# Block sums stored as one run per partition, row records loaded by word and turned on TensorE

## The chip, the cores and the metric

The kernel runs on one core of a Trainium2 chip. A core has TensorE (PE; its weight loads are listed as PEld), VectorE (DVE), ScalarE (ACT), GpSimd (POOL) and SyncE (SP, which here only issues DMAs), a scratch memory of 128 partitions (SBUF), the accumulators that TensorE writes (PSUM), and 16 DMA engines that all queues share. The metric is the device time of one execution in microseconds (us), the median of several runs; lower is better.

## The reference, cut to what matters

A graph layer on 6250 nodes and 200,000 edges sorted by destination, and then a small mixture of experts. Only the graph layer is touched by the change.

```python
def _L0_gnn_ref(x, W, a_src, a_dst, edge_W, edge_b, bias, edge_attr, edge_index):
    h = (x @ W.T).reshape(n, H, D)                       # H = 8 heads of D = 32
    src, dst = (edge_index[0], edge_index[1])
    h_src, h_dst = h[src], h[dst]
    alpha = jnp.einsum('ehd,hd->eh', h_src, a_src) + jnp.einsum('ehd,hd->eh', h_dst, a_dst)
    enc = jax.nn.relu(edge_attr @ edge_W.T + edge_b).reshape(-1, H, D)
    alpha = alpha + jnp.sum(enc * h_dst, axis=-1)
    alpha = jnp.where(alpha >= 0, alpha, 0.2 * alpha)
    amax = jax.ops.segment_max(alpha, dst, num_segments=n)
    ex = jnp.exp(alpha - amax[dst])
    denom = jax.ops.segment_sum(ex, dst, num_segments=n)
    attn = ex / jnp.maximum(denom[dst], 1e-10)
    out = jax.ops.segment_sum(h_src * attn[..., None], dst, num_segments=n)
    return out.reshape(n, H * D) + bias
x = x + _L0_gnn_ref(_layernorm(x), ...)
x = x + _L0_ffn_ref(_layernorm(x)[None], ...)[0]
```

## The kernel before

Four parts follow one another. `prologue` projects the nodes into a table in device memory (`t_node_rows`, 272 floats a node) and sorts the edges into rows of W = 4 slots, each row with edges of one destination. 128 rows make a block, there are 440 blocks. For each row it stores a record of five words: four source ids and the place of the row's node in a window of 128 nodes (`t_block_rows`, tile `ro`). `edge_loop` does the edges, `merge_blocks` joins the sums of nodes that lie in two blocks, `epilogue` fetches each node's sum, divides it and runs the experts.

`edge_loop` is what the change is about. It takes STEPS = 110 steps of Q = 4 blocks, and all its buffers have two slots (RING = 2), so that loads for step q+2 go into the slot that step q leaves. Each engine has its own program, written out by hand in the order in which it runs; they meet at semaphores alone.

- SP, in `body(q)`: `store(q-1)` (L813) writes the sums of the last step, 128 partitions x 4 blocks x 264 floats, after the last copy of sums on ACT (L982). Then `load(q+2)`: `load_rows` (L784, the records), `load_attr` (L792, three DMAs of edge attributes), `load_windows` (L807, four windows of the node table, each after a register load of its base) and `load_flags` (L800, four).
- POOL, in `gather(q)`: 16 indirect DMAs (L856), one for each block and slot, each of which fetches 128 rows of the node table by the ids in the record. The four of block b wait until the step before last has weighed its block b (L1077), for the buffer.
- ACT and PE make the nodes' rows for each block (`front`): ACT makes a one-hot matrix (L943, L947), PE turns it (L871), ACT copies it (L954), PE encodes the attributes (L880) and picks the nodes from the window (L885), ACT copies the result (L963). The next block's L943 stands behind this copy.
- DVE multiplies the encoded attributes with that copy (L1032), adds them up (L1036), makes the scores of the step (L1044 to L1052), runs two scans over the rows (L1059, L1064; PE turns the rows for them, L891, and back, L896), subtracts the tops (L1070), and weighs the gathered rows (L1077) once ACT has taken the exponential (L969).
- PE adds up the weighed rows for each block (`add_up`, L904, 4 of these a block), and ACT copies the sums (L982).

The two transfers that the change touches, and their access patterns, are these:

```python
rows = scr["block_rows"].rearrange("(n q) (r w) -> n r q w", q=Q, w=W + 1)
sp.dma_start(rec[:, q.par, :, :], v).then_inc(s_rec[q.par], 16)            # L784
rows = scr["sums"][0:BLOCKS * P, :].rearrange("(n q p) e -> n p q e", q=Q, p=P)
sp.dma_start(v, sums[:, q.par, :, :]).then_inc(s_stored[q.par], 16)        # L813
```

In both, a partition's four blocks lie apart in device memory. So one transfer is 128 x 4 = 512 pieces: of 5 words (20 bytes) in the record load, and of 264 floats (1056 bytes) in the store. A window's 128 pieces have 1088 bytes each.

Of the kernel before, what the change touches and what calls it, by code (L numbers as in the profile page):

```python
# [8 lines left out]
P = 128  # L9
# [98 lines left out]
def prologue(nc, a, scr, keep):  # L108

    with Scope(nc) as m:  # L110
# [21 lines left out]
        row_at = m.sb("row_at", [P, GROUPS])  # L132
        base = m.sb("base", [P, GROUPS])
        base_mod, base_tile = keep["base_mod"], keep["base_tile"]
        tiny = m.sb("tiny", [P, 4])
        ro = m.sb("ro", [P, P, W + 1])
# [57 lines left out]
            dummy_made dummy_stored bias_loaded""".split()  # L194
# [29 lines left out]
        def _(sp):  # L224
# [46 lines left out]
            for g in range(GROUPS):  # L271
# [3 lines left out]
                sp.dma_start(scr["block_rows"][b0:b0 + n, :], ro[0:n, :, :].rearrange("p r w -> p (r w)")).then_inc(s["table_stored"], 16)  # L275
# [17 lines left out]
        def _(pool):  # L293
# [7 lines left out]
            for g in range(GROUPS):  # L301
# [8 lines left out]
                           allow_small_or_imprecise_dtypes=True).then_inc(s["consts_made"], 1)  # L310
            nc.gpsimd.iota(block_f[:, :], pattern=[[P, GROUPS]], base=1, channel_multiplier=1,
# [173 lines left out]
        def _(dve):  # L485
# [116 lines left out]
            def expand(g):  # L602
# [36 lines left out]
                link(nc.vector.tensor_scalar(ro[:, :, 0:W].bitcast(I32), away.rearrange("p (r k) -> p r k", k=W), float(DUMMY), None, ALU.add))  # L639
# [7 lines left out]
                nc.vector.tensor_scalar(ro[:, :, W], place, -1.0, 1.0, ALU.mult, ALU.add)  # L647
# [23 lines left out]
            link(nc.vector.tensor_tensor(item_to[:, :, 1], item_to[:, :, 1], row_at[:, :], ALU.add))  # L671
            nc.vector.tensor_copy(item_i[:, :, 1], item_to[:, :, 1]).then_inc(s["items_made"], 1)
            nc.vector.tensor_copy(item_i[:, :, 0], row_at[:, :]).then_inc(s["items_made"], 1)
# [39 lines left out]
def edge_loop(nc, a, scr, keep):  # L713

    with Scope(nc) as m:
        rec = m.sb("rec_in", [P, RING, Q, W + 1])
        rec_i = rec[:, :, :, :].bitcast(I32)
# [25 lines left out]
        p_rowT, p_back = p_turn[0:Q * H, 0:P], p_turn[:, 2 * P:2 * P + Q * H]  # L743
        row_of = lambda v: v.rearrange("p (q h) -> p q h", q=Q)
# [7 lines left out]
        names = """waited_by_pe waited_by_pool ones_set apart hot turned hotT picked near enc prod dots raw full score row_top rowT run tops back below  # L752
# [1043 lines left out]
```

## Time and profile before

| | |
|---|---|
| Time, median of 3 runs | 4180.87 us (4165.67 to 4185.18) |
| The profiled execution: time, and span of the trace | 4159.17 us, 4157.4 us |
| Granted TensorE clock, mean | 0.734 |
| PE, PEld busy | 58%, 39% |
| DVE, ACT, POOL busy | 57%, 24%, 48% |
| DMA queue q0 (POOL's gathers), q1 (SP's and ACT's) | 25.6%, 14.8% of 16 engines' span |
| The loop of 110 steps | from about 399 to 3571 us |

Each row of a timeline is an instruction or a run of equal ones: start and duration in us, engine, line, operation, tiles, shapes, and in brackets how long the engine had been idle before it and what ended that. An "SPq" row is the issue of a DMA, not its data. PE's ends are modelled from its starts; when a result really was there is seen at the engine that waited for it. "remote" is a wait whose end came from an update that no instruction's recorded end explains.

### The profile page before, as it was taken

What the parts mean: (1) busy time and instruction counts of PE and PEld (TensorE: products, weight loads), DVE (VectorE), ACT (ScalarE), POOL (GpSimd) and SP (SyncE); (2) the same over time, 40 slices, a digit from 0 to 9 for tenths busy, and PEclk for the clock granted to TensorE, in tenths of its full rate; (3) what the DMA queues carried; (4) which work ended last, traced back from release to release, by engine and by line L of the source; (5) the groups of instructions that cost most, each with busy time, mean ns of one, the idle gap of its engine ahead of it and who ended that gap; (6) DMA issues with size and microseconds to landing.
All of it is one profiled execution on the core that took longest, in us unless ns stands there. A gap on an engine that the chain in (4) does not pass through costs nothing. (4 is left out here: it accounts for less than half of the span.)

```text
span 4157.4 us, 45593 instructions
## 1 busy us (share of the span) xinstructions
PE 2392.0 (58%) x8886; PEld 1609.8 (39%) x8886; DVE 2354.5 (57%) x3523; ACT 992.1 (24%) x3079; POOL 2016.2 (48%) x2041
## 2 busy tenths in 40 slices
PE   3300556566566565565565665665656656416998
PEld 2200334333343343343343343433433433204887
DVE  7596556556556565565565565565655555443223
ACT  4300222222222222222222222222222222124332
POOL 2411555565555555555555655655556555244200
PEclk9755677776777777777777777767767777656999
DMA  7201444444444444444444444444444498320000
GB/s 240 76 30 46 114 125 115 124 124 115 125 122 118 125 123 120 126 122 118 124 115 124 126 117 124 124 113 125 117 122 124 115 118 113 52 66 23 13 20 29
DMA packets 322416, 437.60 MB, mean 105 GB/s; under 512 B 115526, under 2 KB 257832, under 8 KB 322132
## 3 DMA queue, kind: packets, MB, share of 16 engines
q0 software_dynamic: 90000, 262.14, 25.6%
q1 hardware_dynamic: 231540, 174.91, 14.8%
q10 hardware_dynamic: 848, 0.26, 0.0%
q14 instruction: 21, 0.17, 0.0%
q8 instruction: 7, 0.11, 0.0%
HBM read 351.33 MB, written 85.74 MB: 105 GB/s over the span
## 5 line engine op out<-in xcount | busy, mean ns | idle before, releaser
L856 POOL DMA_INDIRECT src_in<-t_node_rows,rec_in x1760 | 1800.8, 1023 | 1369.2 <-DVE weighted L1077 806.8
L1032 DVE SCALAR_TENSOR_TENSOR prod<-p_enc,near 128x512 f32<-128x512 f32 x880 | 566.4, 685 | 1224.6 <-ACT near L963 734.1
L904 PE MATMUL p_sum<-weighted,hot 128*128 128x264 f32 x3520 | 1021.8, 453 | 34.4 <-DVE weighted L1077 34.2
L871 PE MATMUL p_pick<-ident,hot 128*128 128x128 f32 x440 | 162.6, 370 | 1310.6 <-ACT hot L947 883.0
L904 PEld LDWEIGHTS p_sum<-weighted,hot 128*128 128x128 f32 x3520 | 794.5, 229 | 284.5 <-issue 114.6
L871 PEld LDWEIGHTS p_pick<-ident,hot 128*128 128x128 f32 x440 | 68.5, 156 | 1467.8 <-ACT hot L947 1011.1
L1036 DVE TENSOR_REDUCE dots<-prod 128x32 f32<-128x1024 f32 x440 | 536.9, 1220 | 15.2
L885 PE MATMUL p_pick<-win,hotT 128*128 128x272 f32 x880 | 439.9, 593 | 160.3 <-issue 119.6
L1077 DVE TENSOR_TENSOR weighted<-src_in,weighted 128x1024 f32<-128x1024 f32 x440 | 521.8, 1226 | 0.4 <-ACT weighted L969 0.4
L963 ACT COPY near<-p_pick 128x272 f32<-128x272 f32 x440 | 169.9, 386 | 1246.6 <-remote 726.1
L982 ACT COPY sums<-p_sum 128x264 f32<-128x264 f32 x440 | 166.9, 379 | 780.7 <-PE p_sum L904 524.7
L880 PE MATMUL p_enc<-expander,attrT 30*128 30x256 bf16 x1760 | 349.8, 331 | 0.3 <-DMA attrT<-t_block_attr 0.3
L885 PEld LDWEIGHTS p_pick<-win,hotT 128*128 128x128 f32 x880 | 175.2, 249 | 294.8 <-issue 235.8
L943 ACT ACTIVATE apart<-node_at,rec_in 128x128 f32<-128x128 f32 x440 | 175.3, 398 | 255.7 <-DMA rec_in<-t_block_rows 255.7
L880 PEld LDWEIGHTS p_enc<-expander,attrT 30*128 30x128 bf16 x1760 | 170.9, 120 | 99.0 <-issue 54.2
L954 ACT COPY hotT<-p_pick 128x128 f32<-128x128 f32 x440 | 117.6, 267 | 369.4 <-PE p_pick L871 162.2
L1482 PE MATMUL p_up<-x2T,w 128*128 (+2 forms) x800 | 175.9, 379 | 9.0 <-DMA b<-in_L_ffn_b 9.0
L1492 PE MATMUL p_y<-w,act_h 128*128 128x256 f32 x784 | 173.2, 379 | 0.0
L1482 PEld LDWEIGHTS p_up<-x2T,w 128*128 128x128 f32 x800 | 151.4, 192 | 29.7 <-DMA b<-in_L_ffn_b 9.1
L1492 PEld LDWEIGHTS p_y<-w,act_h 128*128 128x128 f32 x784 | 148.9, 190 | 20.2
L1685 DVE TENSOR_TENSOR acc<-acc,p_y 128x256 f32 (+1 forms) x49 | 20.6, 421 | 218.6 <-PE p_y L1492 216.2
L947 ACT ACTIVATE hot<-apart 128x128 f32<-128x128 f32 x440 | 136.1, 309 | 23.2
(293 smaller groups left out, 1639.5 us busy)
## 6 DMA issues: line engine op xcount, KB each, us to landing
win<-t_node_rows SPq DMA_DIRECT2D x440, 136.0 KB
t_block_sums<-sums SPq DMA_DIRECT2D x110, 528.0 KB
src_in<-t_node_rows,rec_in POOLq DMA_INDIRECT x1760
attrT<-t_block_attr SPq DMA_DIRECT2D x330, 36.0 KB
flags_in<-t_block_flags SPq DMA_DIRECT2D x440, 4.0 KB
t_node_rows<-out_rows SPq DMA_DIRECT2D x49, 136.0 KB, 1.7
x<-in_x SPq DMA_DIRECT2D x4, 1536.0 KB, 25.7
out_x<-x SPq DMA_DIRECT2D x48, 128.0 KB
```

Source lines behind the costliest of these rows:

```text
L856: pool.indirect_dma_start(src[:, q.par, b, k, :], None, scr["rows"], bass.IndirectOffsetOnAxis(ap=rec_i[:, q.par, b, k:k + 1], axis=0)).th ...
L871: nc.tensor.transpose(p_hotT, hot[:, q.par, b, :], keep["ident"][:, :]).then_inc(s["turned"], 1)
L880: last = nc.tensor.matmul(p_enc[(PAIRS * b + half) % len(p_enc)][:, j, :], slots, keep["expander"][:, :], start=True, stop=True)
L885: nc.tensor.matmul(p_near, hotT[:, b % 2, :], win[:, q.par, b, :], start=True, stop=True).then_inc(s["picked"], 1)
L904: last = nc.tensor.matmul(p_sum[b % 2][:, 0:ROW], hot[:, q.par, b, :], weighted[:, b, k, :], start=(k == 0), stop=(k == W - 1))
L943: nc.scalar.activation(apart[:, :], keep["node_at"][:, :], ACT.Abs, bias=rec[:, q.par, b, W:W + 1]).then_inc(s["apart"], 1)
L963: nc.scalar.copy(near[:, q.par, b, :], p_near).then_inc(s["near"], 1)
L1032: nc.vector.scalar_tensor_tensor(prod[:, b % 2, 2 * half:2 * half + 2, :], p_enc[(PAIRS * b + half) % len(p_enc)][:, :, :], 0.0, near[:, q ...
L1036: nc.vector.tensor_reduce(dots[:, q.par, b, :, :].rearrange("p k h -> p (k h)"), prod[:, b % 2, :, :].rearrange("p k (h d) -> p (k h) d", ...
L1077: nc.vector.tensor_tensor(heads(weighted[:, b, :, 0:D]), heads(src[:, q.par, b, :, 0:D]), spread(weighted[:, b, :, D:ROW], HD), ALU.mult). ...
L1482: last = nc.tensor.matmul(p_up[n % 4][:, 0:cols], w1[:, k, i, f * P:(f + 1) * P], x, start=(i == 0), stop=(i == 1))
L1492: last = nc.tensor.matmul(p_y[u][:, :], act_h[:, b, n, u * P:(u + 1) * P], w2[:, k, f, :], start=(n == 0), stop=(n == TOPK * hidden - 1))
```

## The change

The store writes each partition's four blocks as one run: row `(n p q)` of `t_block_sums` now holds block q of partition p, where it was `(n q p)`. That is 128 pieces of 4224 bytes. All that reads these sums by index gets new numbers: `item_of` in `prologue`, and in `merge_blocks` the jumps between blocks (`gain`) and `node_id`.

The records are stored word by word, so that a step's records are 20 rows (4 blocks x 5 words) of 128 floats. SP loads them as 20 partitions of 512 bytes (`recT`) and does this at the head of its body, ahead of the store. PE turns them into PSUM (`turn_rec`, two steps ahead, in `turn_rows`), and DVE copies them out (`keep_rec`, between the two scans), the ids as integers and the node places as floats. POOL and ACT wait for these copies (`rec`) instead of the DMA.

```diff
@@ prologue
-                link(nc.vector.tensor_scalar(ro[:, :, 0:W].bitcast(I32), away.rearrange("p (r k) -> p r k", k=W), float(DUMMY), None, ALU.add))
+                link(nc.vector.tensor_scalar(ro[:, 0:W, :].rearrange("p k r -> p r k"), away.rearrange("p (r k) -> p r k", k=W), float(DUMMY), None, ALU.add))
...
-            link(nc.vector.tensor_tensor(item_to[:, :, 1], item_to[:, :, 1], row_at[:, :], ALU.add))
+            link(nc.vector.tensor_scalar(in_step[:, :], in_step[:, :], Q - 1, None, ALU.bitwise_and))
+            link(nc.vector.tensor_copy(tiny[:, 0:1], in_step[:, :]))
+            link(nc.vector.tensor_scalar(tiny[:, 1:2], tiny[:, 0:1], float(1 - P), None, ALU.mult))
+            link(nc.vector.tensor_scalar(sums_at[:, :], row_at[:, :], tiny[:, 1:2], None, ALU.add))
+            link(nc.vector.scalar_tensor_tensor(item_to[:, :, 1], item_to[:, :, 1], float(Q), sums_at[:, :], ALU.mult, ALU.add))
@@ edge_loop, SP
             def load_rows(q):
                 if q.since(RING):
-                    before = q.prev().prev()
-                    for b in range(Q):
-                        sp.wait_ge(s_src[q.par][b], 16 * W * q.turn)
-                    sp.wait_ge(s["hot"], Q * (before.s + 1))
-                rows = scr["block_rows"].rearrange("(n q) (r w) -> n r q w", q=Q, w=W + 1)
-                sp.dma_start(rec[:, q.par, :, :], v).then_inc(s_rec[q.par], 16)
+                    sp.wait_ge(s["rec_up"], q.prev().s)
+                rows = scr["block_rows"].rearrange("(n q) (w r) -> n (q w) r", q=Q, r=P)
+                sp.dma_start(recT[:, q.par, :], block_of(rows, q.s)).then_inc(s_rec[q.par], 16)
...
-                rows = scr["sums"][0:BLOCKS * P, :].rearrange("(n q p) e -> n p q e", q=Q, p=P)
-                sp.dma_start(v, sums[:, q.par, :, :]).then_inc(s_stored[q.par], 16)
+                rows = scr["sums"][0:BLOCKS * P, :].rearrange("(n p q) e -> n p (q e)", q=Q, p=P)
+                sp.dma_start(block_of(rows, q.s), sums[:, q.par, :, :].rearrange("p q e -> p (q e)")).then_inc(s_stored[q.par], 16)
             def load(q):
-                load_rows(q)
                 load_attr(q)
                 load_windows(q)
                 load_flags(q)
             def body(q):
+                load_rows(q.next().next())
                 if q.since(1):
                     store(q.prev())
                 load(q.next().next())
@@ edge_loop, POOL and ACT
-                pool.wait_ge(s_rec[q.par], 16 * (q.turn + 1))
+                pool.wait_ge(s["rec"], 2 * q.s + 2)
@@ edge_loop, PE
+            def turn_rec(q):
+                pe.wait_ge(s_rec[q.par], 16 * (q.turn + 1))
+                if q.since(1):
+                    pe.wait_ge(s["rec"], 2 * q.s)
+                    nc.tensor.sem_inc(s["waited_by_pe"], 1)
+                nc.tensor.transpose(p_rec.rearrange("p q w -> p (q w)"), recT[:, q.par, :], keep["ident"][0:Q * (W + 1), 0:Q * (W + 1)]).then_inc(s["rec_up"], 1)
+
-            def turn_rows(q):
-                pe.wait_ge(s["row_top"], q.s + 1)
+            def turn_rows(q, more):
                 if q.since(1):
                     pe.wait_ge(s["below"], q.s)
+                if more:
+                    turn_rec(q.next().next())
+                pe.wait_ge(s["row_top"], q.s + 1)
@@ edge_loop, DVE
+            def keep_rec(q):
+                dve.wait_ge(s["rec_up"], q.s + 1)
+                nc.vector.tensor_copy(ids[:, q.par, :, :], p_rec[:, :, 0:W]).then_inc(s["rec"], 1)
+                nc.vector.tensor_copy(node[:, q.par, :], p_rec[:, :, W]).then_inc(s["rec"], 1)
@@ merge_blocks
-            nc.vector.tensor_scalar(gain[:, 1:BLOCKS], gain[:, 1:BLOCKS], float(P), None, ALU.add).then_inc(s["gain"], 1)
+            nc.vector.tensor_scalar(gain[:, 1:BLOCKS], gain[:, 1:BLOCKS], float(Q), 1.0, ALU.mult, ALU.add).then_inc(s["gain"], 1)
+            dve.wait_ge(s["gain"], 3)
+            nc.vector.tensor_scalar(gain[:, Q:BLOCKS:Q], gain[:, Q:BLOCKS:Q], float(P * Q - Q), None, ALU.add).then_inc(s["gain"], 1)
+            nc.vector.memset(low[:, :], -BIG).then_inc(s["low"], 1)
```

How instructions stand on an engine is shown by rows of its program (line, operation, tiles, shape; "ISA" and "REGISTER_ALU" are waits and register work). On SP, in the loop's body, the stretch from the store to the attributes' load was this before:

```order
L813 ISA
L813 DMA t_block_sums<-sums 128x4x264
L780 ISA
L781 ISA
L784 ISA
L784 DMA rec_in<-t_block_rows 128x4x5
L788 REGISTER_ALU
L792 ISA
L792 DMA attrT<-t_block_attr 9x2048 x3
```

The same stretch after the change (L792 is now the records' load, L820 the store, L800 the attributes; the four windows and the flags follow as before):

```order
L792 ISA
L792 DMA rec_in<-t_block_rows 20x128
L818 ISA
L820 ISA
L820 DMA t_block_sums<-sums 128x1056
L796 REGISTER_ALU
L800 ISA
L800 DMA attrT<-t_block_attr 9x2048 x3
```

The record load moved from behind the store to ahead of it, and the waits for gathers (L780) and one-hots (L781) are gone from SP.

On DVE, the rows around the two scans in one step before the change, where `p_turn` is the PSUM tile that PE turns into:

```order
L1052 TENSOR_REDUCE row_top<-score 128x32
L1032 SCALAR_TENSOR_TENSOR prod<-p_enc,near 128x512 x2
L1036 TENSOR_REDUCE dots<-prod 128x32
L1059 SCALAR_TENSOR_TENSOR run<-flags_in,p_turn 32x128
L1064 SCALAR_TENSOR_TENSOR tops<-flags_in,run 32x128
```

And after it:

```order
L1072 TENSOR_REDUCE row_top<-score 128x32
L1052 SCALAR_TENSOR_TENSOR prod<-p_enc,near 128x512 x2
L1056 TENSOR_REDUCE dots<-prod 128x32
L1084 SCALAR_TENSOR_TENSOR run<-flags_in,p_turn 32x128
L1076 CAST edge_ids<-p_turn 128x16
L1077 COPY row_node<-p_turn 128x4
L1091 SCALAR_TENSOR_TENSOR tops<-flags_in,run 32x128
```

Two small copies now stand between the scans; on PE one more matmul (`p_turn<-ident,rec_in 128x20`) stands just ahead of the one that turns `row_top`.

## Rows read from the trace of the kernel before

**Rows 1.** Page, DMA packets of the span, and the chosen DMA issues of its part 6

```profile
DMA packets 322416, 437.60 MB, mean 105 GB/s; under 512 B 115526, under 2 KB 257832, under 8 KB 322132
...
win<-t_node_rows SPq DMA_DIRECT2D x440, 136.0 KB
t_block_sums<-sums SPq DMA_DIRECT2D x110, 528.0 KB
```

**Rows 2.** The store's issues: duration ns min/median/max, first and last start us

```profile
L813 SPq DMA_DIRECT2D t_block_sums<-sums x110: 372/428/437, 471.4 to 3571.2; - x110
```

**Rows 3.** Timeline of one step, 2007 to 2038 us, chosen rows of all engines

```profile
2007.65 0.43 SPq L813 DMA_DIRECT2D t_block_sums<-sums  x1
...
2009.63 0.71 SPq L784 DMA_DIRECT2D rec_in<-t_block_rows  x1
...
2012.84 1.28 PE L885 MATMUL p_pick<-win,hotT 128*128 128x272 f32 x2 [1.13 <-issue]
...
2013.89 3.50 SPq L792 DMA_DIRECT2D attrT<-t_block_attr  x3
...
2016.38 0.95 POOL L856 DMA_INDIRECT src_in<-t_node_rows,rec_in  x1 [0.30 <-issue]
2019.59 3.88 SPq L807 DMA_DIRECT2D win<-t_node_rows  x4
2019.65 0.39 ACT L963 COPY near<-p_pick 128x272 f32<-128x272 f32 x1 [6.87 <-remote]
...
2024.65 1.14 POOL L856 DMA_INDIRECT src_in<-t_node_rows,rec_in  x1 [7.33 <-DVE weighted L1077]
...
2037.21 0.43 SPq L813 DMA_DIRECT2D t_block_sums<-sums  x1
```

**Rows 4.** Same timeline: block sums on PE twice, and one block's chain on ACT

```profile
2023.97 6.36 PE L904 MATMUL p_sum<-weighted,hot 128*128 128x264 f32 x16 [0.30 <-DVE weighted L1077]
...
2030.64 0.40 ACT L943 ACTIVATE apart<-node_at,rec_in 128x128 f32<-128x128 f32 x1
...
2032.81 3.72 PE L904 MATMUL p_sum<-weighted,hot 128*128 128x264 f32 x16
2033.09 0.39 ACT L963 COPY near<-p_pick 128x272 f32<-128x272 f32 x1 [0.95 <-PE p_pick L885]
```

**Rows 5.** Waits of the whole span: us in total, times, longest

```profile
ACT near L963 <- remote: 726.1, 138, 8.9
```

**Rows 6.** Page, part 5, the groups that fill a step

```profile
L856 POOL DMA_INDIRECT src_in<-t_node_rows,rec_in x1760 | 1800.8, 1023 | 1369.2 <-DVE weighted L1077 806.8
L1032 DVE SCALAR_TENSOR_TENSOR prod<-p_enc,near 128x512 f32<-128x512 f32 x880 | 566.4, 685 | 1224.6 <-ACT near L963 734.1
...
L1036 DVE TENSOR_REDUCE dots<-prod 128x32 f32<-128x1024 f32 x440 | 536.9, 1220 | 15.2
...
L1077 DVE TENSOR_TENSOR weighted<-src_in,weighted 128x1024 f32<-128x1024 f32 x440 | 521.8, 1226 | 0.4 <-ACT weighted L969 0.4
```

**Rows 7.** Timeline of SP alone at the loop's start, 399 to 425 us

```profile
402.33 3.73 SPq L807 DMA_DIRECT2D win<-t_node_rows  x4
...
407.54 0.40 SPq L784 DMA_DIRECT2D rec_in<-t_block_rows  x1
...
410.26 12.61 SPq L807 DMA_DIRECT2D win<-t_node_rows  x3
```

**Rows 8.** Timeline of POOL in the epilogue: the first of 49 gathers of the sums

```profile
3638.51 1.00 POOL L1432 DMA_INDIRECT acc<-t_block_sums,sum_at  x1 [0.16 <-issue]
```

**Rows 9.** Timeline of DVE beside those gathers, two rows of its loop over the nodes

```profile
3657.37 0.74 DVE L1588 BATCH_NORM_STATS2 e_stats<-x  x2
...
3672.79 0.42 DVE L1579 TENSOR_TENSOR fresh<-acc,inverse 128x256 f32 x1 [5.17 <-issue]
```

**Rows 10.** Groups, 1000 to 2000 us: the small turn on PE, a small DVE operation from PSUM

```profile
L1070 DVE TENSOR_TENSOR below<-score,p_turn 128x128 f32<-128x128 f32 x35 | 9.7, 277 | 0.0
L891 PE MATMUL p_turn<-ident,row_top 128*32 128x128 f32 x35 | 9.5, 272 | 0.0
```

More of the change, by code:

```diff
@@ L751, in edge_loop @@
         s_stored = [m.sem(f"s_sums_stored{i}") for i in range(RING)]
-        names = """waited_by_pe waited_by_pool ones_set apart hot turned hotT picked near enc prod dots raw full score row_top rowT run tops back below
+        names = """waited_by_pe waited_by_pool ones_set rec_up rec apart hot turned hotT picked near enc prod dots raw full score row_top rowT run tops back below
             weight weighted summed sums tops_kept""".split()
@@ L836, in _ @@
             for k in range(RING):
+                load_rows(straight(k))
+            for k in range(RING):
                 load(straight(k))
@@ L909, in body @@
                 h = Q // 2
-                turn_rows(q)
+                turn_rows(q, ahead > 1)
                 if ahead:
@@ L927, in last @@
                 body(straight(STEPS - 1), 0)
+            turn_rec(straight(0))
+            turn_rec(straight(1))
             for b in range(Q):
@@ L939, in make_hot @@
                 if b == 0:
-                    act.wait_ge(s_rec[q.par], 16 * (q.turn + 1))
+                    act.wait_ge(s["rec"], 2 * q.s + 2)
                 if b or q.since(1):
                     act.wait_ge(s["hot"], n)
-                nc.scalar.activation(apart[:, :], keep["node_at"][:, :], ACT.Abs, bias=rec[:, q.par, b, W:W + 1]).then_inc(s["apart"], 1)
+                nc.scalar.activation(apart[:, :], keep["node_at"][:, :], ACT.Abs, bias=node[:, q.par, b:b + 1]).then_inc(s["apart"], 1)
                 act.wait_ge(s["apart"], n + 1)
@@ L1059, in scan @@
                 nc.vector.tensor_tensor_scan(run[:, :], flags[:, q.par, 0:P], p_rowT, -BIG, ALU.add, ALU.max).then_inc(s["run"], 1)
+                if more:
+                    keep_rec(q.next().next())
                 dve.wait_ge(s["run"], q.s + 1)
@@ L1078, in weigh, with body @@
                                         spread(weighted[:, b, :, D:ROW], HD), ALU.mult).then_inc(s["weighted"], 1)
-            def body(q, ahead=True):
+            def body(q, ahead=True, more=True):
                 n = q.next()
@@ L1086, in body @@
                         front(n, b)
-                scan(q)
+                scan(q, more)
                 if ahead:
@@ L1103, in last @@
             def last():
-                body(straight(STEPS - 2))
-                body(straight(STEPS - 1), False)
+                body(straight(STEPS - 2), more=False)
+                body(straight(STEPS - 1), False, False)
             nc.vector.memset(attrT[:, :, :, :], 1.0).then_inc(s["ones_set"], 1)
@@ L1109, in _ @@
             dve.wait_ge(s["ones_set"], 2)
+            keep_rec(straight(0))
+            keep_rec(straight(1))
             for b in range(Q):
@@ L1143, in merge_blocks @@
         past = m.sb("past", [NT, P])
+        low = m.sb("low", [NT, P])
         sum_row = m.sb("sum_row", [NT, P])
@@ L1150, in merge_blocks @@
         p_at = m.ps("p_at", [P, NT])
-        names = """tops_in parts_in consts even_i even gain gains_up gains hots past_up past carry at_made at_up sum_at flags unlike ends away to twice run tops
+        names = """low tops_in parts_in consts even_i even gain gains_up gains hots past_up past carry at_made at_up sum_at flags unlike ends away to twice run tops
             fall scale turned scales made chained whole last_up over put""".split()
@@ L1297, in _ @@
         def _(pe):
-            pe.wait_ge(s["gain"], 3)
+            pe.wait_ge(s["gain"], 4)
             for g in range(GROUPS):
```

32 lines of the change are left out of this document (19 added, 13 removed).

## The prediction, made before the changed kernel had run

> **What bounds the kernel now.** I read the page first, for where the time is, then the store's issues for the length of a step, then one step's timeline, then the waits, and last two places outside the steady loop where the same engines run under other conditions.
>
> The 110 stores start between 471.4 and 3571.2 us [rows 2], so a step takes (3571.2 - 471.4) / 109 = 28.4 us, and the loop is three quarters of the span. No engine fills a step. The costly groups [rows 6] give DVE 4 x (2 x 0.685 + 1.220 + 1.226) = 15.3 us, and with its seven small operations of about 0.3 us [rows 10] some 17.5. POOL's 16 gathers take 16 x 1.023 = 16.4 us, and its idle time that is not a wait for DVE, (1369.2 - 806.8) / 1760 = 0.32 us for each gather, makes this 21.5 us; by the gather at 2016.38, 0.95 us behind 0.30 of issue, it is 20.0 [rows 3]. The other 806.8 us, 7.3 a step, POOL waits for DVE's weighing of the buffer [rows 3, 6]. So POOL is not the bound yet, but it is next.
>
> What takes the rest is in the timeline of one step [rows 3]. At 2007.65 SP issues the store. PE's pick that is listed at 2012.84 should be done at 2014.12, but ACT copies its result at 2019.65; the row says "remote" behind 6.87 us of idleness, and these waits add up to 726.1 us over 138 times [rows 5]. SP goes slowly at the same time: the record load comes 1.6 us after the store's issue ended, and the windows' register loads begin only when the stretch ends, at 2019.59. POOL's gathers run on at their own pace; the last starts at 2016.38, and 3 us after it PE, ACT and SP are quick again. I call 2007.65 to 2019.6 the slow stretch. DVE loses it too, since it waits for ACT's copy.
>
> Its price: from the store to the end of ACT's copy at 2020.04 two blocks' copies were made, in 12.4 us. When the engines are quick, one block goes from L943 at 2030.64 to the end of L963 at 2033.48, in 2.84 us [rows 4]. The first of the two blocks was at its pick already, about 1.2 us from the end. So the work was worth 1.2 + 2.84 = 4.1 us, and the stretch loses 8.3 us a step. It also costs clock: four fifths of a step later 16 block-sum matmuls take 6.36 us, right after the idleness, where they take 3.72 later [rows 4].
>
> What starts it is the question. Two places help. At the loop's start [rows 7] SP issues four windows (4 x 128 pieces, 544 KB, [rows 1]) in 3.73 us beside running gathers, and nothing is slow. At 407.54 it issues a record load, 512 pieces of 20 bytes, only 10 KB, and from then on three windows take 12.61 us. So it isn't the bytes, and not a DMA of SP beside gathers as such, but a DMA with 512 pieces. The second place speaks against so simple a rule: in the epilogue, gathers run without a pause from 3638.51 [rows 8], SP is idle, DVE makes two operations in 0.74 us at 3657.37, and later waits 5.17 us for nothing that the profile shows before one operation [rows 9]. There, some 19 us of gathers without a pause were enough.
>
> **The change, part by part.** It takes 384 pieces from each store and 492 from each record load. That is 876 x 110 = 96,360 of the 322,416 packets [rows 1]; the windows keep their 512 a step.
>
> *The slow stretch.* If it goes, the step falls by 8.3 us to 20.1, or lower with the clock. POOL's gathers then bound it: 20 us by their quiet pace, 21.5 by the group's mean. Both ends are known from rows; I take 21.2, nearer to the mean, since one gather a step takes up to 2 us whatever else happens, and 0.8 us for the turn from one buffer to the next, where POOL still waits for DVE. That is 22.0 us a step, 6.4 less. The sum: 109 x 6.4 = 698 us.
>
> *New work in the loop.* PE turns 20 x 128 floats, at most like the turn of `row_top`, 0.27 us. DVE makes two copies from PSUM of at most 0.28 us each [rows 10]: 0.55. If all of it lay on the path, it would cost 0.82 x 110 = 90 us. DVE then has 17.5 + 0.55 = 18.1 us of work in a step of 22, so I take nothing; the cover is POOL's gathers, and without that cover the 90 us are the upper end. The waits that come with it: `turn_rec` waits for a load that SP issued at the head of its body, most of a step earlier, and for DVE's copies of the step before; behind it on PE stand `turn_rows` and the scans. POOL's new wait (`rec`) ends in the scan, and the gathers behind it wait for the later weighing anyhow. Neither should be last.
>
> *The record load ahead of the store on SP.* One issue of 0.4 us [rows 7] ahead of the store, in a time when SP would only wait for the last sums. Nothing. SP loses its waits for gathers and one-hots, which had ended by then.
>
> *The store itself.* The same 528 KB [rows 1] in longer pieces. Nobody waits for its data but the slot's next user, two steps later. Nothing.
>
> *Prologue and merge.* Five more small DVE operations and a strided write for each of four groups, two more in the merge; at 0.3 us each [rows 10] about 3 us, which I leave out. The first two steps may gain up to some 20 us from the missing record load at 407.54; it is left out as well and widens the low end.
>
> The sum is 4159 - 698 = 3461 us against the profiled execution (4159.17; its span is 4157.4). The median of the runs shown lies 0.5% higher, so the forecast is 3461 x 1.005 = 3480.
>
> **A rule that speaks against it.** The trace shows engines that are slow without waiting for any of its data [rows 3]. The Trainium skill (DMA: Bandwidth & Descriptors, Why small descriptors are slow (HBM only)) puts the cost of a short piece at about three cycles of the DMA engine and 32 bytes of descriptor traffic, nothing that would hold an engine's instructions; by it the pieces are hidden behind computing and the change is worth nothing, 4180. The trace has something that the rule doesn't speak of, the slow stretch, and this is the third rival below.
>
> **The rivals.**
>
> *The stretch comes back in part.* If POOL no longer pauses, gathers run in an unbroken row as in the epilogue [rows 9], and the windows, now issued right behind the store, run beside them instead of in the pause. Then something else starts the stretch, but it feeds on itself: the slower DVE, the longer POOL pauses, and the pause ends it. For it: the epilogue. Against: four windows beside gathers did nothing for 5 us [rows 7]. A step of 25.2 us, in the middle between 23.0 and 26.7, gives 4159 - 109 x 3.2 = 3810, and 3830 as a median; the ends give 3590 and 3990.
>
> *Nothing changes.* If the store's 528 KB or its writes to device memory start the stretch and not its pieces, or if it is hidden as in the rule, the step stays at 28.4 and the time at 4160 to 4200. For it: nearly every stretch begins at the store, not the record load. Against: the record load alone did it at 407.54 [rows 7].
>
> *Slower: the early record load starts the stretch earlier.* It is issued behind the last flags, about 2025 us in the step shown, when gathers have just begun again (2024.65). If any DMA of its kind beside gathers is enough, even with 20 pieces, the stretch runs from there to the next store at 2037.21 too, 12.2 us more. At the loss rate of now, 8.3 / 11.9 = 0.7, this is 8.5 us a step and 4159 + 927 = 5086 us. It decides from the point where 20 pieces act like 512; against it stand the windows of 128.
>
> **How the numbers follow.** The stretch goes and POOL bounds the loop: 0.50, with 3340 (20.9 us a step and the first steps' gain) to 3590 (the new work in the path, 22.8 us, and a little). In part: 0.30, 3590 to 3990. Nothing changes: 0.12. Slower: 0.08. The likeliest case's time is 3480. The range 3340 to 3990 takes in the first two, 8 in 10. Faster by over 0.5% (about what a measurement of this kernel tells from no change) is 0.82 with a little of the third case, the same 0.09, slower 0.09.
>
> **What would show it.** Right: stores 22 us apart; "remote" waits before ACT's L963 down from 726 us to under 150; POOL's wait for the weighing down from 807 us to under 150; the windows issued within 2 to 6 us of the store; the granted clock above 0.734. In part: "remote" waits stay, but begin later than the store and POOL's waits lie between. Wrong: stores 28 us apart and the ACT copy 5 us late right behind a store of 128 pieces. For the new work: PE's 128 x 20 turn under 0.3 us, and the second scan at most 0.6 us later than the first's end. What would make it wrong above all is that the pieces of these two transfers aren't what the slow stretch needs.

## The result, and the profile after

The changed kernel took 4224.48 us in the median of 4 runs (4220.74 to 4233.47), the kernel before 4176.28 beside it (4 runs, 4165.67 to 4185.18): ratio 1.0132, 95% interval 1.0113 to 1.015. It is slower, where 3480 was forecast. The profiled execution took 4224.42 us, with a span of 4222.7.

The page of the changed kernel, its DMA packets and three groups of part 5:

```profile
DMA packets 225396, 437.60 MB, mean 104 GB/s; under 512 B 58546, under 2 KB 146732, under 8 KB 225112
...
L865 POOL DMA_INDIRECT src_in<-t_node_rows,edge_ids x1760 | 1795.8, 1020 | 1436.4 <-DVE weighted L1104 896.8
...
L983 ACT COPY near<-p_pick 128x272 f32<-128x272 f32 x440 | 169.9, 386 | 1267.2 <-remote 743.5
...
L901 PE MATMUL p_turn<-ident,rec_in 20*128 20x20 f32 x110 | 25.8, 235 | 257.7 <-DMA rec_in<-t_block_rows 257.7
```

Each line of a group gives busy time in us and the mean of one in ns, then the engine's idle time before it and what ended most of that. Against [rows 1] 97,020 packets are gone, and not a byte. Against [rows 5, 6] the waits stayed: 743.5 us for "remote" at ACT's copy of `near` (726.1 before), 896.8 us of POOL's for the weighing (806.8). The store's issues, where [rows 2] stood:

```profile
L820 SPq DMA_DIRECT2D t_block_sums<-sums x110: 333/384/388, 474.3 to 3635.6; - x110
```

A step takes (3635.6 - 474.3) / 109 = 29.0 us, 0.56 more than before; that is 61 of the 65 us that the span grew by. One step's timeline, chosen rows, answers to [rows 3]:

```profile
2010.00 1.15 POOL L865 DMA_INDIRECT src_in<-t_node_rows,edge_ids  x1 [8.27 <-DVE weighted L1104]
...
2020.55 0.23 PE L901 MATMUL p_turn<-ident,rec_in 20*128 20x20 f32 x1
...
2020.72 0.28 PE L909 MATMUL p_turn<-ident,row_top 128*32 128x128 f32 x1
...
2021.04 0.41 DVE L1084 TENSOR_TENSOR_SCAN run<-flags_in,p_turn 32x128 f32<-32x128 f32 x1 [0.81 <-PE p_turn L909]
...
2021.28 0.39 SPq L820 DMA_DIRECT2D t_block_sums<-sums  x1
2021.37 0.14 DVE L1076 CAST edge_ids<-p_turn 128x16 int32<-128x16 f32 x1
2021.44 0.14 DVE L1077 COPY row_node<-p_turn 128x4 f32<-128x4 f32 x1
...
2021.63 0.41 DVE L1091 TENSOR_TENSOR_SCAN tops<-flags_in,run 32x128 f32<-32x128 f32 x1
...
2026.33 0.39 ACT L983 COPY near<-p_pick 128x272 f32<-128x272 f32 x1 [4.92 <-remote]
...
2029.98 0.95 POOL L865 DMA_INDIRECT src_in<-t_node_rows,edge_ids  x1 [0.30 <-issue]
...
2033.16 1.16 SPq L815 DMA_DIRECT2D win<-t_node_rows  x2
```

The store of 128 pieces is issued at 2021.28, and behind it the near copy starts only after 4.92 us of idleness for "remote"; SP gets from the attributes to the windows only at 2033.16, when the gathers (last one at 2029.98) are over. So the slow stretch is there as before. New is what stands ahead of it: the records' turn at 2020.55 is in front of `row_top`'s on PE, and the two copies are between the scans on DVE. The copies cost next to nothing there. The scans start 0.59 us apart, and in the kernel before, with nothing between them, they were as far apart:

```profile
2036.68 0.41 DVE L1059 TENSOR_TENSOR_SCAN run<-flags_in,p_turn 32x128 f32<-32x128 f32 x1 [0.54 <-PE p_turn L891]
...
2037.28 0.41 DVE L1064 TENSOR_TENSOR_SCAN tops<-flags_in,run 32x128 f32<-32x128 f32 x1 [0.19 <-issue]
```

Over all steps the median distance is 0.60 us in both kernels.

### The profile page after: what moved, and what is told of

The parts are those of the page before. It is cut to its first block and busy times, and to the rows that moved or that the text cites. A ratio compares the mean times of both kernels' runs of the same rounds, so it can differ in the third digit from the quotient of the medians.

```text
span 4222.7 us, 46308 instructions
## 1 busy us (share of the span) xinstructions
PE 2450.8 (58%) x8996; PEld 1624.0 (38%) x8996; DVE 2366.7 (56%) x3749; ACT 1001.7 (24%) x3079; POOL 2011.9 (48%) x2042
## 2 busy tenths in 40 slices
DMA packets 225396, 437.60 MB, mean 104 GB/s; under 512 B 58546, under 2 KB 146732, under 8 KB 225112
## 3 DMA queue, kind: packets, MB, share of 16 engines
q0 software_dynamic: 90000, 262.14, 25.2%
## 5 line engine op out<-in xcount | busy, mean ns | idle before, releaser
L865 POOL DMA_INDIRECT src_in<-t_node_rows,edge_ids x1760 | 1795.8, 1020 | 1436.4 <-DVE weighted L1104 896.8
L983 ACT COPY near<-p_pick 128x272 f32<-128x272 f32 x440 | 169.9, 386 | 1267.2 <-remote 743.5
L889 PE MATMUL p_enc<-expander,attrT 30*128 30x256 bf16 x1760 | 364.5, 342 | 0.5 <-DMA attrT<-t_block_attr 0.5
L963 ACT ACTIVATE apart<-node_at,row_node 128x128 f32<-128x128 f32 x440 | 175.3, 398 | 257.0 <-DVE row_node L1077 257.0
L901 PE MATMUL p_turn<-ident,rec_in 20*128 20x20 f32 x110 | 25.8, 235 | 257.7 <-DMA rec_in<-t_block_rows 257.7
```

Source lines behind the costliest of these rows:

```text
L865: pool.indirect_dma_start(src[:, q.par, b, k, :], None, scr["rows"], bass.IndirectOffsetOnAxis(ap=ids[:, q.par, b, k:k + 1], axis=0)).then ...
L889: last = nc.tensor.matmul(p_enc[(PAIRS * b + half) % len(p_enc)][:, j, :], slots, keep["expander"][:, :], start=True, stop=True)
L963: nc.scalar.activation(apart[:, :], keep["node_at"][:, :], ACT.Abs, bias=node[:, q.par, b:b + 1]).then_inc(s["apart"], 1)
L983: nc.scalar.copy(near[:, q.par, b, :], p_near).then_inc(s["near"], 1)
```

## The experiments

Each group of experiments ran on one chip, with the kernel before beside it. The chips turned out to differ, so they have letters; A is that of the times above. A ratio is always to the kernel before on the same chip, and a "burst" is a step's sixteen gathers, which POOL issues 1.25 us apart with a pause behind them.

| chip | kernel before, us (runs) | experiments |
|---|---|---|
| A | 4176 (4) | |
| B | 4258 (17) | `e1` to `e4` |
| C | 3430 (7) | `e5` to `e8` |
| D | 4283 (17) | `e9` to `e12` |
| E | 4223 (7) | `e13` to `e16` |
| F | 3419 (23) | `e17`, `e18` |

**Which half of the change costs: `e1_store_only`, `e2_rec_only`.** The first is the kernel before with the store's layout changed, the second the changed kernel with that undone:

```diff
-rows = scr["sums"][0:BLOCKS * P, :].rearrange("(n q p) e -> n p q e", q=Q, p=P)
+rows = scr["sums"][0:BLOCKS * P, :].rearrange("(n p q) e -> n p (q e)", q=Q, p=P)
```

> The kernel before with only the store's half of the change: block sums stored as 128 runs of 4224 bytes, the record load still 512 pieces of 20 bytes, nothing new in the loop on PE or DVE. The changed kernel showed the slow stretch of each step starting behind the 128-piece store just as it had behind the 512-piece one, and steps 0.5 us longer. Theory A (the number of store pieces costs nothing here, and the +1.3% comes from turning the records on PE): 4176 +/- 10 us, ratio 0.997 to 1.003, stretch still in every step, ACT's wait of the near copy put to remote 700 to 760 us. Rival B (the store's new layout is itself what costs, through the writes or the epilogue): at least half of the +1.3% here, 4200 us or more.

> The changed kernel with the store put back to 512 pieces of 1056 bytes: only the record load by word, its turn on PE and the two copies on DVE. Theory A (before the stretch the turn of the records stands ahead of the turn of row_top on PE, +0.27 us, and the two copies stand between the scans on DVE, +0.15 us; 0.42 us a step x 110 = 46 us, and some more by the start): ratio 1.009 to 1.015, 4215 to 4240 us, the two scans 0.55 to 0.65 us apart at their starts. Rival B (the store costs the time): under 4195 us.

Measured: 4254.98 us, ratio 0.9997 (0.998 to 1.0013), and 4398.87 us, ratio 1.0326 (1.0304 to 1.0348). 384 pieces fewer in each store are worth nothing, and the whole loss is in the records' half. But both of theory A's numbers for it fail: by the stores' issues the steps are 30.57 us in `e2` against 29.28 in `e1`, three times the 0.42 us that theory A gave. Of that 0.42, the 0.15 for the copies between the scans was never there, as shown above.

**Is it SP's transfers, or the gathers: `e3_no_gathers`, `e4_sp_in_pause`.** The edits, `e3`'s first, from the third step on (its waits for the gathers are made to fit, and the source rows are wrong):

```diff
-for k in range(W):
+for k in range(0 if q.since(RING) else W):
     pool.indirect_dma_start(...)
```

```diff
 def body(q):                      # of SP
+    for b in range(Q):
+        sp.wait_ge(s_src[1 - q.par][b], 16 * W * (q.next().turn + 1))
     if q.since(1):
         store(q.prev())
```

> The kernel before, with GpSimd's gathers issued in the first two steps only; later steps reuse the rows that these left in src_in (source rows of all later steps are wrong, everything else is done as before, the 512-piece store and load included). If gathers are a necessary part of the slow stretch: it is gone in every step, ACT's near copy waits under 100 us for remote, steps are set by DVE's 16.4 us of work and its waits, 17 to 21 us, total about 2900 to 3450 us. If the stretch comes from the store or the other SP transfers alone (writes to DRAM, DMA of many pieces): it stays, with PE and SP instructions 0.7 us apart behind each store, and steps stay over 24 us.

> The kernel before, with one wait more: SP holds all of a step's transfers (store, records, attributes, windows, flags) until the step's sixteen gathers have landed, so that none of SP's DMAs runs beside a gather. Theory S (a transfer of SP's beside gathers starts the slow stretch): no stretch, steps 21 to 23 us, 3400 to 3600 us; ACT's remote wait under 100 us. Theory G (the gathers start it by themselves once they have run about 11 us without a pause): the stretch stays, from about 11 us after the first gather of a burst to its end, PE and DVE slow in it with SP idle, steps 27 us or more, 4100 us or more, since the late transfers add waits.

Measured: 3280.76 us and 4239.93 us (one run each). Without gathers the step is 20.36 us and the stretch gone. With SP's transfers held back until a burst is over, the stretch stays; the transfers now reach only some 5 us into the next burst, and the timeline of `e4` shows the stretch long behind them:

```profile
2003.92 1.15 POOL L858 DMA_INDIRECT src_in<-t_node_rows,rec_in  x1 [7.60 <-DVE weighted L1079]
...
2006.72 1.82 SPq L800 DMA_DIRECT2D flags_in<-t_block_flags  x4
...
2015.93 0.38 ACT L984 COPY sums<-p_sum 128x264 f32<-128x264 f32 x1 [1.35 <-PE p_sum L906]
...
2016.58 0.27 ACT L956 COPY hotT<-p_pick 128x128 f32<-128x128 f32 x1 [0.27 <-PE p_pick L873]
...
2021.02 0.39 ACT L965 COPY near<-p_pick 128x272 f32<-128x272 f32 x1 [4.18 <-remote]
...
2023.90 0.94 POOL L858 DMA_INDIRECT src_in<-t_node_rows,rec_in  x1 [0.30 <-issue]
...
2027.24 0.27 SPq L813 DMA_DIRECT2D t_block_sums<-sums  x1
2027.44 0.39 ACT L965 COPY near<-p_pick 128x272 f32<-128x272 f32 x1 [4.19 <-remote]
```

SP issues nothing between the flags of 2006.72 (1.82 us long) and the store of 2027.24. Yet ACT and PE are quick until 2015.93, 12 us behind the first gather, and then two near copies in a row come after 4.2 us of idleness for "remote"; the second 2.6 us after the last gather's end. Theory S, of which the prediction's is a narrower form, is dead: with the gathers there, the stretch needs no transfer of SP's, and without them it does not come. Nor does a record load start it: at the loop's start, right behind the one of 407.54 that the prediction took for the cause [rows 7], SP of the kernel before was still quick, with three issues in 1.13 us.

```profile
407.98 1.13 SPq L792 DMA_DIRECT2D attrT<-t_block_attr  x3
```

**A break in the bursts: `e5_break_mid`, `e6_break_each`, `e7_half_gathers`, `e8_after_break_mid`.** `e5` adds a wait to the kernel before and `e8` to the changed one, `e6` for `b in (1, 2, 3)`; `e7` gathers only `k` of 0 and 1 from the third step on, so half its source rows are wrong:

```diff
+if b in (2,):
+    pool.wait_ge(s_src[q.par][b - 1], 16 * W * (q.turn + 1))
 for k in range(W):
     pool.indirect_dma_start(...)
```

> The kernel before with one wait more on GpSimd: after the second of the four groups of gathers of a step it waits until these eight have landed, so that a burst of sixteen (20.0 us without a break) becomes two of eight (10 us each) with a break of about 2 us. With all of SP's transfers moved out of the gathers, the slow stretch still began 11 to 12 us into each burst. Theory R (an unbroken run of gathers of over about 11 us brings it on, and a drained queue resets it): the stretch is gone from the steps, ACT's near copy waits under 150 us for remote, steps 22.5 to 25 us, 3600 to 3900 us. Rival C (a break of 2 us resets nothing, the gathers' sum since the long pause counts): the stretch starts as before, the step is longer by the break, 30 to 31 us, ratio 1.02 to 1.06.

> The same with a wait for the landing after each group of four gathers: three breaks of about 2 us in a step. Theory R: no stretch; GpSimd's 16 x 1.25 + 3 x 2 + 2 us bound the step at 28 us, so the time is 4050 to 4260 us though PE, DVE and SP are never slow. Rival C: stretch from the third group on, steps over 31 us, over 4400 us.

> The kernel before with eight gathers a step in place of sixteen (the third and fourth row of each group of four are gathered in the first two steps alone and reused, so the source rows of half the edges are wrong; all else is done). A burst is 10 us. Theory R: no stretch, steps set by DVE and its waits as in the kernel whose later steps have no gathers (3281 us): 3280 to 3500 us. Rival (any gathers beside the 512-piece store or load bring it on): a stretch of some us stays behind each store, over 3550 us.

> The changed kernel with the same one wait of GpSimd's in the middle of each burst. Theory R with the records' turn at 0.42 us a step only where PE and DVE bound the step: if GpSimd bounds the steps once the stretch is gone, the change's new work is hidden and this kernel stands within 0.5% of the kernel before with the break; if PE, ACT and DVE still bound the step, it is 40 to 60 us slower than that. Rival C: 4300 us or more.

Measured on chip C: 3750.71 (1.0935, 1.0904 to 1.0967), 4215.74, 3220.02 and 3748.32 us (1.0927, 1.0895 to 1.0958). The times are those of theory R or (`e7`) just below, and say nothing for it, because here the kernel before takes 3430 us. Chip C has no slow stretch to take away. What these runs do show: a break costs some 2.9 us a step where POOL is the bound (25.2 us a step by `e5`'s stores, against 22.3 of `e17` below, the changed kernel on chip F), and the changed kernel is level with the one before when both have it.

**The same kernels on another chip: `e9_after_again`, `e10_before_again`, `e11_break_mid_again`, and `e12_turn_late`.** The first three are kernels already told. The last is the changed kernel with the turn moved:

```diff
 def turn_rows(q, more):
-    if more:
-        turn_rec(q.next().next())
...
     turn_back(q)
     for b in range(h, Q):
         front(n, b)
+        if b == h and ahead > 1:
+            pe.wait_ge(s["below"], q.s + 1)
+            turn_rec(n.next())
...
     fall(q)                       # DVE; no longer in scan
+    if more:
+        keep_rec(n.next())
```

> The changed kernel as it is, once more, on the chip that this call gets. The kernel before took 4176 and 4258 us on two chips and 3430 us on a third, so the slow stretch is not there on every chip. Theory P (whether the stretch occurs is a property of the chip or of its place, the change has no hand in it): where the kernel before takes about 3430 us, this one takes 3400 to 3450 us, ratio 0.99 to 1.01, since GpSimd's 20.0 us of gathers and 2 us of waits set the step and hide the records' turn; where it takes over 4100 us, ratio 1.01 to 1.02. Rival: the stretch is brought on by the change's store or load on a chip where the kernel before is free of it, ratio over 1.05.

> The kernel before, for a trace on the chip of this call. Theory P: if the time is about 3430 us, no instruction of SP or PE goes at 0.7 us beside the gathers, ACT's near copy waits under 150 us for remote, steps are 21.5 to 22.5 us (20.0 us of gathers and a pause of about 2 us); if it is over 4100 us, the stretch stands from 11 us into each burst as in the first trace. Rival: the quick chip has the stretch too and gains elsewhere (a higher granted clock, faster gathers).

> The kernel before with the one wait of GpSimd's for the landing in the middle of each burst, a second time: the chip it had before was free of the stretch, so it could only cost there (1.0935). On a chip with the stretch, theory R (an unbroken run of over about 11 us brings it on): 3720 to 3800 us as on the quick chip, ratio 0.87 to 0.90. Rival C (the break resets nothing): ratio 1.02 to 1.10. On a quick chip again 1.09 and nothing learned.

> The changed kernel with the records' turn moved off the chain row_top, turn, two scans: on PE behind the third block's encoding and pick, with a wait for below, on DVE the two copies behind the subtraction that makes below. Theory A (the turn ahead of row_top's and the copies between the scans cost 0.42 us a step on the chain): on a chip with the stretch 40 to 60 us faster than the changed kernel in this call, ratio to before 0.998 to 1.005. On a quick chip, where GpSimd sets the step: within 0.3% of the changed kernel. Rival (the cost comes from more instructions in the slow stretch, not from their place): no faster than the changed kernel on a chip with the stretch, or slower, as the turn now lies inside it.

Measured on chip D, where the kernel before takes 4283 us: 4418.04 (1.0319, 1.0292 to 1.0347), 4293.31, 4039.08 (0.9442, 0.9412 to 0.9473) and 4276.4 us (0.9986, 0.9969 to 1.0003). The changed kernel loses more than the 1 to 2% expected, and the moved turn takes it all back, 142 us where 40 to 60 were expected: the same work at another place costs nothing. Since `e12` has neither transfer in 512 pieces, its 0.9986 also shows no gain from the record load's pieces. A step of `e9` shows what the turn can cost at the old place:

```profile
2045.19 0.23 PE L901 MATMUL p_turn<-ident,rec_in 20*128 20x20 f32 x1
...
2045.92 0.39 SPq L820 DMA_DIRECT2D t_block_sums<-sums  x1
...
2047.28 0.41 DVE L1084 TENSOR_TENSOR_SCAN run<-flags_in,p_turn 32x128 f32<-32x128 f32 x1 [2.41 <-remote]
...
2047.88 0.41 DVE L1091 TENSOR_TENSOR_SCAN tops<-flags_in,run 32x128 f32<-32x128 f32 x1
...
2057.44 0.39 ACT L983 COPY near<-p_pick 128x272 f32<-128x272 f32 x1 [9.20 <-remote]
...
2066.36 1.15 POOL L865 DMA_INDIRECT src_in<-t_node_rows,edge_ids  x1 [11.59 <-DVE weighted L1104]
```

The burst of gathers began at 2033.87. `row_top`'s turn followed the records' turn on PE in time, but DVE's first scan starts after 2.41 us of idleness (0.81 in the step of chip A), now itself for "remote", the near copy after 9.20 us, and the pause behind the burst is 11.59 us. I took two means over the bursts of sixteen gathers that begin between 600 and 3400 us: the start of the second scan, from the burst's first gather, and POOL's pause behind the burst.

| kernel, chip | bursts | second scan, us | pause, us |
|---|---|---|---|
| before, A | 98 | 11.8 | 7.5 |
| changed, A | 96 | 12.2 | 8.2 |
| before, D | 94 | 12.0 | 8.8 |
| changed, D | 90 | 12.7 | 9.9 |
| turn moved, D | 94 | 12.0 | 8.6 |
| store only, B | 95 | 11.9 | 8.5 |
| records only, B | 91 | 12.6 | 9.7 |

The scans stand about where the stretch sets in, and where they come 0.4 to 0.7 us later the pause is 0.7 to 1.2 us longer. 1.1 us x 109 = 120 of `e9`'s 135 us more. The mean hides two kinds of step, and the one shown is of the dear kind: pauses of 10 us and over are 7 of 94 in the kernel before on D, 39 of 90 in the changed one and 8 of 94 with the turn moved; on B they are 4 of 95 with the store's half and 36 of 91 with the records'; on A 0 of 98 and 3 of 96. In `e9` these pauses are 11.1 us on average and the others 9.0. So most of the loss on B and D is in steps where a small delay pushes more work into the stretch, and chip A, where the scans come earliest, has few of these and loses least. Why A has so few is read from these counts and not tested.

The break (`e11`) fell between both theories. It gains 5.6% and not 10 to 13. It does not cut the bursts as meant: the groups behind one break often run on into the next step's first two without a pause, sixteen in a row again. And 2.7 us without gathers don't reset what came before (`e11`, POOL, SP and ACT):

```profile
1982.85 0.94 POOL L859 DMA_INDIRECT src_in<-t_node_rows,rec_in  x1 [2.67 <-DMA src_in<-t_node_rows,rec_in]
...
1985.63 6.51 SPq L807 DMA_DIRECT2D win<-t_node_rows  x2
...
2002.87 0.95 POOL L859 DMA_INDIRECT src_in<-t_node_rows,rec_in  x1 [0.30 <-issue]
...
2005.90 0.38 ACT L985 COPY sums<-p_sum 128x264 f32<-128x264 f32 x1 [7.51 <-remote]
```

Two windows take 6.51 us only 2.8 us after the gathers resumed (four take 3.88 in the pause, [rows 3]). So "over 11 us without a break" is not the whole condition.

**What of the gathers: `e13_half_again`, `e14_narrow`, `e15_direct`, and `e16_late_break`.** `e13` is `e7` again; `e16` is `e12` with the break. The other two, both from the third step on and with wrong source rows (`e15` loads the same 2048 neighbouring rows in each step):

```diff
-to, table = src[:, q.par, b, k, :], scr["rows"]
+to, table = src[:, q.par, b, k, 0:TABROW // 2], scr["rows"].rearrange("n (h e) -> (n h) e", h=2)
```

```diff
-pool.indirect_dma_start(src[:, q.par, b, k, :], None, scr["rows"], ...)
+pool.dma_start(src[:, q.par, b, k, :], scr["rows"][n:n + P, :])
```

> The kernel before with eight gathers a step in place of sixteen (third and fourth row of each group gathered in the first two steps alone, the source rows of half the edges are wrong), a second time: its first chip was free of the stretch (3220 us there). On a chip with the stretch: theory R (it takes a run of over about 11 us) 3220 to 3350 us and no SP or PE instruction at 0.7 us; rival (some share of time under gathers is slow, whatever the run's length): some slow instructions in each burst of 10 us, 3400 us or more.

> The kernel before with sixteen gathers a step of 544 bytes a row in place of 1088 (a half row at a wrong place of the table; the other half of src_in stays from the first two steps): same number of gathers and descriptors, half the bytes. If the descriptors or GpSimd's issuing bring the stretch on: within 1.5% of the kernel before on the same chip, stretch as long. If the bytes do (DMA engines or DRAM busy with gathers): the stretch shrinks or goes, over 5% faster.

> The kernel before with the gathers of all later steps replaced by plain loads of 128 neighbouring rows of the same table, issued from the same engine to the same tiles (same bytes and rows a step, no indices; the source rows are wrong). If it is the indexed issuing that slows the other engines: no stretch, steps 20 to 23 us, 3300 to 3500 us. If any such stream of loads from that queue does it: stretch as before, over 4000 us.

> The changed kernel with both the moved turn of the records (0.9986 of the kernel before on a chip with the stretch) and the break in the middle of each burst (0.9442 alone on the kernel before). If the two are independent: ratio 0.935 to 0.955 on a chip with the stretch, 1.08 to 1.10 on one without. If with shorter stretches PE is no longer late when the turn comes, or the turn falls into the break: within 0.5% of the break alone; else slower than 0.96.

Measured on chip E (before: 4223 us): 3285.72, 4215.14, 3282.26 (one run each) and 4047.87 us (0.9584, 0.9568 to 0.96). Half the bytes change nothing. Eight gathers a step bring the time of none (3281, on chip B). And the direct loads do so with all the bytes and packets of the kernel before; its page:

```profile
DMA packets 322417, 437.60 MB, mean 133 GB/s; under 512 B 115527, under 2 KB 257833, under 8 KB 322133
...
L858 POOL DMA_DIRECT2D src_in<-t_node_rows x1728 | 916.6, 538 | 1303.8 <-DVE weighted L1081 1218.1
...
L967 ACT COPY near<-p_pick 128x272 f32<-128x272 f32 x440 | 169.9, 386 | 570.7 <-PE p_pick L889 538.7
```

That is 133 GB/s, and "remote" is down to 22.5 us in two waits at the near copy. So neither the load on the DMA engines nor the count of packets slows the other engines; what is left is something in the gathers by index. Two things aren't separated. Direct loads are issued in 16 x 0.54 = 8.6 us a step, and eight gathers in about 10, so both also keep POOL's issuing short. And the direct loads read neighbouring rows, the gathers scattered ones. `e16` fell between its expectations: it is behind the 0.955 of independent gains and 1.5% behind the break alone on chip D; whether the moved turn costs that, or the chip, is open.

**A chip without the stretch: `e17_after_third`, `e18_late_third`.** The changed kernel and `e12` once more.

> The changed kernel as it is, on the chip that this call gets. Where the kernel before takes about 3430 us: ratio 0.995 to 1.005, since the gathers' 20.0 us and 2 us of waits set the step. Where it takes over 4100 us: ratio 1.01 to 1.035, as on the two chips before (1.013 and 1.032).

> The changed kernel with the records' turn moved behind the third block's pick and below. Where the kernel before takes about 3430 us: within 0.5% of it and of the changed kernel. Where it takes over 4100 us: 0.995 to 1.002 of the kernel before and 1 to 3% faster than the changed kernel. Rival (the first pair was chance): no difference from the changed kernel.

Measured on chip F: 3423.55 us, ratio 1.0024 (1.0008 to 1.004), and 3427.19, ratio 1.0022 (1.0009 to 1.0035). The changed kernel there, groups and store:

```profile
L865 POOL DMA_INDIRECT src_in<-t_node_rows,edge_ids x1760 | 1857.5, 1055 | 623.0 <-issue 498.7
...
L983 ACT COPY near<-p_pick 128x272 f32<-128x272 f32 x440 | 169.4, 385 | 652.3 <-PE p_pick L894 652.3
```

```profile
L820 SPq DMA_DIRECT2D t_block_sums<-sums x110: 332/384/388, 450.9 to 2884.8; - x110
```

ACT's copy waits for PE's pick alone (652.3 of 652.3 us), POOL is idle mostly for its own issue (498.7 of 623.0 us), and a step takes 22.3 us. The bursts run into one another here, 1664 gathers in a row with no pause of 2 us, and still none of SP's register operations takes over 0.6 us. POOL is the bound, the place of the turn makes no difference, and the records' work is hidden but for some 5 us in all.

A count in the traces sums it up: SP's register moves and arithmetic that took over 0.6 us each. They are 459 in the kernel before and 440 in the changed one on A, 463, 461 and 498 in `e9`, `e10` and `e12`, 451 with half rows, 430 and 457 with the break (`e11`, `e16`), 46 with SP in the pause, where SP hardly runs in the stretch, 8 to 10 with no gathers, eight gathers or direct loads, and 0 in all six traces of C and F.

## Why the prediction was wrong

- **"Not the bytes, and not a DMA of SP beside gathers as such, but a DMA with 512 pieces."** This step failed. The store's pieces are worth nothing (`e1`, 0.9997), with the record load's gone too nothing is gained (`e12`, 0.9986), and with SP's transfers out of the later part of the gathers the stretch is still there (`e4`). So the 8.3 us a step that the change was to save were not its to save; the step grew by 0.56 us. The evidence at the loop's start [rows 7] had another reading: the gathers began at 401.85, with the four windows, and the three slow ones came 8 us later; time had passed, not only a record load. The epilogue [rows 9], which the prediction noted and then outvoted, was the true case: SP idle, gathers without a pause, engines slow.
- **The price of the stretch, 8.3 us a step, and POOL as the bound behind it, 22.0 us.** Both right in size, where the stretch is absent: steps are 20.4 us without gathers (`e3`), where the prediction had 20.1, and 22.3 with them on a chip without the stretch (`e17`); the kernel before takes 3419 and 3430 us on such chips. 109 x 6.1 = 665 us of the difference to chip A lie in the loop. The rest is outside, where the prediction allowed 20 us at the start: the first store comes at 450.9 instead of 474.3, and from the last store to the end it is 550 instead of 587 us, with the epilogue's 49 gathers in it. So 3480 is near the time of a kernel without the stretch, but the change does not remove the stretch.
- **New work taken as nothing, 90 us as its upper end.** The durations were right: 235 ns for the turn and 2 x 0.14 us for the copies. The cover was not. It was POOL's gathers, and the prediction named the loss without that cover as 0.82 us a step at most. On A the loop's loss was 0.56 us a step, within that bound; on D it is 1.07 us, above it, by the long pauses counted above. "Neither should be last" was wrong for PE: the turn stood ahead of `row_top`'s, on the chain to the scans.
- **The record load ahead of the store, and the rival that it starts the stretch early.** Nothing was right: it is issued at the head of the burst and the engines stay quick; steps are 29.0 us and not the 28.4 + 8.5 = 36.9 of this rival.
- **The rival "nothing changes", 0.12.** It held for the pieces of both transfers; its 4160 to 4200 us missed the 4224 by the new work. The rule that stood beside it, the Trainium skill's on short pieces (DMA: Bandwidth & Descriptors, Why small descriptors are slow (HBM only)), gave 4180 for the case that the pieces are hidden; `e1` agrees with it, at 0.9997.
- **The range, 3340 to 3990,** left the result out, since it held the case that the cause is another one at 0.12, and no case in which the new work costs something while the stretch stays. The sign "stores 28 us apart and the ACT copy 5 us late right behind a store of 128 pieces" is what came.
- **Two small misreadings.** The packets that went are 97,020, not 96,360. And SP's register load for the first window stands at 2018.09, inside the stretch; only the windows' issue at 2019.59 is at its end [rows 3]. Neither bears on the forecast.

Open is what in the gathers by index slows the others (the issuing or the scattered reads), whether an unbroken run or its share of the time decides, and why chips C and F are free of it: whether the chip, its place, or what ran beside it was not tried.

## What to carry to other kernels

When engines are slow for no reason that the profile names, look for a place where the suspect is absent and the symptom is there; one such place outweighs several where both occur together. Put new small work where the engine waits anyhow, never ahead of the instruction that a chain of other engines waits for: here the same turn cost 3.2% at one place and nothing at the other, on one chip. And price a change on a second chip before trusting either sign: the same kernel took 3419 to 4283 us, and a break in the gathers gained 5.6% on one chip and lost 9.4% on another, so no version here beats both kernels everywhere.

## What was unexpected of the hardware

- While POOL issues indexed gathers (1.25 us apart), many of SP's instructions take about 0.70 us each, registers' included, and so do DVE's register operations in the epilogue; PE is late with its results (ACT's copy after 4.92 to 9.20 us of idleness in the steps shown). It starts 8 us behind the first gather at the loop's start, some 12 us into a burst in the steps, and 3 us after a pause of 2.67 us (`e11`); it ends within 3 us of the last issue, and POOL keeps its own pace.
- It goes neither by bytes nor by packets: with half the bytes it stays (4215 against 4223 us), and with direct loads of the same 437.60 MB it is gone (3282 us).
- Four of six chips have it and two don't, with medians some 750 to 860 us apart for one kernel; on each chip the runs of one kernel agree within 1%, but for one run on F.
- Without it, POOL's sixteen gathers are the bound at 22.3 us a step (`e17`); with no gathers a step takes 20.4 (`e3`).
